# The first two images reordered, sums written into the low halves, and the middle products laid out row by row

## The chip, the cores and the metric

The kernel runs on one core of a Trainium2 chip. The metric is device time in microseconds for one call. Before the change three runs took 1633.83 to 1634.32 us, median 1634.29.

## The reference

The input x is (32, 256, 28, 28) in fp32. The reference convolves each channel with 12 fixed log-polar masks of 9x9, mixes the 12 results over the channels with a 4x3 convolution (`w_conv1`), adds a 1x1 convolution of x and a bias, normalizes over the batch, adds x and takes the ReLU:

```
xp  = log_pooling(x)                      # 12 mask averages per pixel, as (B, C, 4*H, 3*W)
out = conv(xp, w_conv1, stride (4, 3)) + conv1x1(x, w_center) + b_center
out = (out - mean(out, (0,2,3))) * rsqrt(var(out, (0,2,3)) + 1e-5) * gamma + beta
out = relu(out + x)
```

## The kernel before, in words

**Layout.** The 256 channels are two halves (c) of 128 partitions. A picture lies column by column: 28 columns of H = 28 values. An image is worked through in two halves, step s = 2 x image + c, and each output half o is accumulated in PSUM over both c. Odd and even columns of the output (q) have their own banks: banks 0 to 3 for y, banks 4 to 7 (MBANK on) for the middle products m = 0, 1 of each o. U = 14, HALF = U x H = 392.

**Sums.** VectorE builds for each half, in this order (`image_steps`, line 558): `d`, the differences of columns two apart (L567); D1 and D2, even plus odd and odd minus even columns (L570, L571); V, vertical sums of `d` (L573); then `row3` and `row3v` (L586, L590), `box4` and `box3` (L604, L606), and three pooled pairs: `pooled_sums` 0 and 1 (L610, L612) and the third in two pieces (`short_sum`, L617). row3 needs `row2`, the third pair needs `ends`: both are made by two transfers, a plain load issued by SP (`begin_sum`, L283) and an adding one issued by POOL (`add_from`, L246) that waits for it. The sums stand in buffers `inner` (D1, D2, V) and `pooled` (two slots).

**High and low parts.** Each fp32 operand is a rounded fp32r part plus a rest. ScalarE copies the sum into the first half of `inner_split` or `pooled_split`, which rounds it (`split_inner` L374, `split_pooled` L384); VectorE subtracts that from the sum and writes the rest into the second half (L582, L594 and `lo_of_pooled`, L553). Weights are split the same way (`split_weights`, `lo_of_weights`). A product is three matmuls: high x high, low weights x high, high x low (`products`, L669; L675 to L677).

**TensorE's order** per half (L686 to L731): the middle products of D1 and D2 (for each m, o: the tap in the middle on all 392 columns, and two shifted taps on 378), 36 matmuls; the inner products of V and `d`, 24 of 392 columns; three pooled pairs, 24 of 364 columns each. For c = 0 it waits for `middle_taken` ahead of the middle products and for `y_ready` ahead of the inner ones. It releases `m_done`, `inner_done` (once per half) and `pooled_done` (once per pair).

**The striped layout.** D1, D2 and the middle banks hold two columns interleaved, so that a shift by one row of the picture is a shift by 2 elements within a stripe of 56: 7 stripes of 54 elements are the shifted product. The column pairs are written by VectorE at a step of 2 elements:

```
striped = (STRIPE, STRIPES), (1, 2), (2, H)                 # 56 x 7, 1 x 2, 2 x 28
add(view(inner, D1, *striped), even, odd)
shorter = (STRIPE, STRIPES), (1, SHORTER)                   # 7 runs of 54
```

**Taking an image.** After the middle products of c = 1 ScalarE copies the banks of m = 0 to `m1_copy` (`copy_m1`, L391). In the next image VectorE's `take_middle` (L503) adds and subtracts them with the banks of m = 1, read from PSUM, into `y_stage`, right behind V of c = 0; `take_y` (L515) adds banks 0 to 3 after the first low pooled part. SP then saves y to DRAM (L312). ScalarE measures sum and sum of squares of each y half (`measure`, L398).

**The order on SP** per half (`image_steps`, L301): when row3 is ready, x of the next image; row2's load when the second pooled sum of this half is done; ends' load when the third is; for c = 0 the save of y. At the start: x, both blocks of the first half's weights, row2, ends, x of the second half, its weights, the parameters (L326 to L332). In images 0 and 1 the order is the loop's, with the weights' work put in; `transform_weights(0)` comes first of all. TensorE runs WARM_UP = 20 matmuls on zeros before (L682).

**The tail.** 32 images are finished in two rounds of 16 slots: y and x are loaded, VectorE scales and adds (L662), ScalarE adds the shift and takes the ReLU (L444), and stores. Slots 1 to 15 lie over the buffers of the conv stage, in places of 784 KB (`load_places`, L322), each loaded as soon as what stood there is done with: 4 in `w_stage` once the y save of image 30 has landed, 5 more in `w_first` after the last half but one, and so on (L338 to L350).

Of the kernel before, what the change touches and what calls it, by code (L numbers as in the profile page):

```python
# [7 lines left out]
def conv_bn_relu_program(nc, x, x_wide, w_raw, b_center, gamma, beta, out, y_dram):  # L8
# [22 lines left out]

    STRIPES, STRIPE = U // 2, 2 * H
    SHORTER = STRIPE - 2
# [34 lines left out]
    with ctx:  # L68
# [11 lines left out]
        with ExitStack() as phase1:  # L80
# [7 lines left out]
            w_stage = reused("w_stage", CH * RAW * CHANNELS)  # L88
            w_first = reused("w_first", 2 * TAPS * CHANNELS, F32R)
# [7 lines left out]
            inner = reused("inner", 4 * HALF)  # L97
            pooled = reused("pooled", 2 * PAIR)
# [8 lines left out]
        m1_copy = sb("m1_copy", CH * HALF)  # L107

        D1, D2, VD, SD = 0, HALF, 2 * HALF, 4 * HALF

# [19 lines left out]
        AFTER_STAGE = places_within("w_stage")  # L130
        AFTER_FIRST = places_within("w_first")
        AFTER_SUMS = places_within("pooled")
# [66 lines left out]
        m1_copied = sem("m1_copied")  # L199
# [15 lines left out]
        WARM_UP = 20  # L215
# [60 lines left out]
        def _(sp):  # L276
# [18 lines left out]
            def load_weights(c):  # L295
                for part, (first, end) in enumerate(((0, RAW_OUTER), (RAW_OUTER, RAW))):
                    sp.dma_start(view(w_stage, (c * RAW + first) * CHANNELS, (1, (end - first) * CHANNELS)),
                                 w_raw[:, c, first:end, :].rearrange("p k o -> p (k o)"))\
                        .then_inc(w_loaded[c][part], 16)
# [27 lines left out]
            load_weights(0)  # L327
            begin_sums(0, 0)
            load_x(0, 1)
            load_weights(1)  # L330
# [29 lines left out]
        def _(act):  # L360
# [13 lines left out]
            def split_inner(s):  # L374
                act.wait_ge(v_ready, s + 1)
                wait_from_one(act, inner_done, s)
                nc.scalar.activation(view(inner_split, 0, (1, SD)), view(inner, 0, (1, SD)), ACT.Copy)\  # L377
# [6 lines left out]
            def split_pooled(s, c, j):  # L384
                wait_from_one(act, pooled_done, PAIRS * s - PAIRS + j + 1)
# [22 lines left out]
            def image_steps(image, first=False):  # L408
                for c in range(CH):
                    s = CH * image + c  # L410
                    if c == 0 and not first:
                        copy_m1(image - 1)
# [7 lines left out]
                    for j in range(PAIRS):  # L420
                        split_pooled(s, c, j)
# [353 lines left out]
```

## Time and profile before

| | |
|---|---|
| three runs | 1633.83, 1634.29, 1634.32 us |
| the profiled execution | 1634.39 us, span of its instructions 1632.7 us |
| mean granted TensorE clock | 0.949 |
| TensorE busy | 1459.9 us, 89% |
| VectorE busy | 1421.4 us, 87% |
| ScalarE busy | 639.6 us, 39% |
| POOL busy | 121.3 us, 7% |
| moved by the transfer engines | 268.76 MB |

The profile is one execution recorded in the chip. Busy is the time in which an engine had an instruction running; matmuls overlap, so the distance from the start of one to the start of the next says more of their cost than the duration of one. Times within the trace are counted from the first instruction. The conv stage ends at 1480, the rest is the normalizing tail.

### The profile page before, as it was taken

To read this page: it belongs to the slowest core of one execution; us is meant where nothing else is said; L and a number is where in the kernel's file an instruction comes from. 1 tells how busy PE (TensorE), PEld (TensorE's weight loads), DVE (VectorE), ACT (ScalarE), POOL (GpSimd) and SP (SyncE) were. 2 spreads that over 40 slices of the span, in tenths; PEclk is the share of its full clock that TensorE was granted. 3 is DMA by queue.
4 is the path that set the end of the run, shared out by engine and by line. 5 is a ranking of instruction groups with operands and counts; after the bars stand their busy time and mean duration, and the time that the engine had idled before them with its cause. 6 is when DMAs were issued, how large, how long until landed. Compare 5 with 4: busy or idle time off the path is not lost.

```text
span 1632.7 us, 22865 instructions
## 1 busy us (share of the span) xinstructions
PE 1459.9 (89%) x8468; PEld 1458.6 (89%) x8468; DVE 1421.4 (87%) x1391; ACT 639.6 (39%) x689; POOL 121.3 (7%) x160
## 2 busy tenths in 40 slices
PE   6899999999999999999999999999999999992000
PEld 5899999999999999999999999999999999992000
DVE  7999999999999999999999999999999999986332
ACT  3334434334334343443433334343343333435332
POOL 1000000000000000000000000000000000000000
PEclk8999999999999999999999999999999999996555
DMA  6456554555555555455545555555555455579999
GB/s 200 108 132 146 136 134 126 125 145 127 119 124 133 145 136 137 128 122 143 135 115 120 136 139 136 141 127 128 135 136 122 116 140 133 136 253 420 425 425 400
DMA packets 65352, 268.76 MB, mean 165 GB/s; under 512 B 7616, under 2 KB 7616, under 8 KB 65344
## 3 DMA queue, kind: packets, MB, share of 16 engines
q1 hardware_dynamic: 39744, 160.53, 29.5%
q0 software_dynamic: 20736, 82.45, 26.5%
q10 hardware_dynamic: 4864, 25.69, 3.8%
q14 instruction: 6, 0.05, 0.0%
q8 instruction: 2, 0.03, 0.0%
HBM read 218.07 MB, written 50.58 MB: 165 GB/s over the span
## 4 chain that ended last, share of the span: by engine, by line
PE 86%; DMA 6%; DVE 3%; ACT 2%; another core or an unknown queue 1%; issue 1%; ACTq 0%; SPq 0%; DVEq 0%; POOLq 0%
PE acc L676 29%; PE acc L677 29%; PE acc L675 29%; DMA out<-phase 3%; DMA phase<-y_dram 2%; ACT phase L444 1%; DMA row<-x_wide 1%; DVE pooled L452 1%; DVE pooled_split L453 1%; DVE inner_split L453 0%; ACTq L447 0%; ACT m_copy L403 0%; DVE y_stage L452 0%; DVE row3v L452 0%
## 5 line engine op out<-in xcount | busy, mean ns | idle before, releaser
L387 ACT ACTIVATE pooled_split<-pooled 128x1456 fp32r<-128x1456 f32 x192 | 273.4, 1424 | 609.6 <-DVE pooled L452 609.6
L453 DVE TENSOR_TENSOR pooled_split<-pooled,pooled_split 128x1456 fp32r<-128x1456 f32 x192 | 315.1, 1668 | 0.3 <-ACT pooled_split L387 0.3
L675 PE MATMUL acc<-pooled_split,w_first 128*128 128x364 f32 x768 | 252.7, 329 | 5.1 <-DVE pooled_split L453 5.1
L676 PE MATMUL acc<-pooled_split,w_first 128*128 128x364 f32 x768 | 253.4, 330 | 0.0
L677 PE MATMUL acc<-pooled_split,w_first 128*128 128x364 f32 x768 | 253.4, 330 | 0.0
L677 PE MATMUL acc<-pooled_split,w_outer 128*128 128x364 f32 x768 | 252.8, 329 | 0.0
L676 PE MATMUL acc<-pooled_split,w_outer 128*128 128x364 f32 x768 | 252.5, 329 | 0.0
L675 PE MATMUL acc<-pooled_split,w_outer 128*128 128x364 f32 x768 | 252.0, 328 | 0.0
L675 PE MATMUL acc<-inner_split,w_first 128*128 128x392 f32 (+1 forms) x640 | 219.2, 342 | 13.6 <-DVE inner_split L453 9.3
L677 PE MATMUL acc<-inner_split,w_first 128*128 128x392 f32 (+1 forms) x640 | 218.3, 341 | 0.0
L676 PE MATMUL acc<-inner_split,w_inner 128*128 128x392 f32 (+1 forms) x640 | 218.0, 341 | 0.0
L676 PE MATMUL acc<-inner_split,w_first 128*128 128x392 f32 (+1 forms) x640 | 217.9, 340 | 0.0
L677 PE MATMUL acc<-inner_split,w_inner 128*128 128x392 f32 (+1 forms) x640 | 217.5, 340 | 0.0
L675 PE MATMUL acc<-inner_split,w_inner 128*128 128x392 f32 (+1 forms) x640 | 217.1, 339 | 0.0
L452 DVE TENSOR_TENSOR pooled<-box,row 128x1456 f32<-128x1456 f32 x128 | 208.2, 1667 | 0.0
L453 DVE TENSOR_TENSOR inner_split<-inner,inner_split 128x1568 fp32r<-128x1568 f32 x64 | 114.7, 1792 | 95.7 <-ACT inner_split L377 95.7
L377 ACT ACTIVATE inner_split<-inner 128x1568 fp32r<-128x1568 f32 x64 | 96.9, 1514 | 188.7 <-PE acc L677 167.8
L675 PEld LDWEIGHTS acc<-pooled_split,w_first 128*128 128x128 f32 x768 | 145.0, 189 | 5.4 <-DVE pooled_split L453 5.4
L676 PEld LDWEIGHTS acc<-pooled_split,w_first 128*128 128x128 f32 x768 | 144.7, 188 | 0.0
L677 PEld LDWEIGHTS acc<-pooled_split,w_first 128*128 128x128 f32 x768 | 144.7, 188 | 0.0
L676 PEld LDWEIGHTS acc<-pooled_split,w_outer 128*128 128x128 f32 x768 | 144.5, 188 | 0.0
L677 PEld LDWEIGHTS acc<-pooled_split,w_outer 128*128 128x128 f32 x768 | 144.4, 188 | 0.0
(82 smaller groups left out, 2154.9 us busy)
## 6 DMA issues: line engine op xcount, KB each, us to landing
row<-x_wide SPq DMA_DIRECT2D x64, 558.0 KB, 3.6
row<-x_wide POOLq DMA_DIRECT2D x64, 558.0 KB, 7.3
ends<-x_wide SPq DMA_DIRECT2D x64, 504.0 KB, 4.0
ends<-x_wide POOLq DMA_DIRECT2D x64, 504.0 KB, 5.8
x_pad<-x SPq DMA_DIRECT2D x64, 392.0 KB, 3.1
y_dram<-y_stage SPq DMA_DIRECT2D x31, 784.0 KB, 8.5
phase<-y_dram SPq DMA_DIRECT2D x30, 784.0 KB, 30.8
out<-phase ACTq DMA_DIRECT2D x30, 784.0 KB, 34.4
```

The source lines that it names most:

```text
L377: nc.scalar.activation(view(inner_split, 0, (1, SD)), view(inner, 0, (1, SD)), ACT.Copy)\
L387: nc.scalar.activation(view(pooled_split, 2 * j * PAIR, (1, PAIR)), view(pooled, (PAIRS * c + j) % 2 * PAIR, (1, PAIR)), ACT.Copy)\
L444: nc.scalar.activation(x_slot(d, o), x_slot(d, o), ACT.Relu, bias=bn_shift[:, o:o + 1]).then_inc(relu_done, 1)
L452: add = lambda out_, a, b: nc.vector.tensor_tensor(out_, a, b, ALU.add)
L453: sub = lambda out_, a, b: nc.vector.tensor_tensor(out_, a, b, ALU.subtract)
L675: nc.tensor.matmul(place, hi_w, hi_in, start=start, stop=False)
L676: nc.tensor.matmul(place, lo_w, hi_in, start=False, stop=False)
L677: return nc.tensor.matmul(place, hi_w, lo_in, start=False, stop=stop)
```

## The change

- **Layout.** D1, D2 and the middle banks are row by row: element (h, u) at 14 h + u. A shift by one row is a shift by 14, and a shifted product is one run of 378. VectorE writes D1 and D2 with a step of 14 elements.
- **Copies.** ScalarE copies all four middle banks (`copy_middle`, two instructions of 784 elements), reading PSUM with a step of 14 and writing columns to `m_copy`. `take_middle` is two instructions of 784 elements on SBUF. TensorE waits for `m_copied` in place of `middle_taken`.
- **Freed buffers.** `inner` and `pooled` are gone. Their sums are written into the low halves of `inner_split` and `pooled_split`, and the low part is formed in place. So VectorE waits for `inner_done` and for `pooled_done` of the half before ahead of writing. `spare`, of the same size, lies behind `w_stage`.
- **Order on VectorE.** Images 0 and 1 have orders of their own, with each low part right behind its sum. In the loop: (take_middle,) row3, row3v, boxes, differences, two pooled sums, the low parts of the inner sums, the first low pooled part, (take_y,) the third sum, two low parts.
- **SP.** The second weight block comes behind row2's load; x of the next image waits for V too; one place of the tail is loaded after image 29, two after image 30, and places 3 to 6 behind the last y save. WARM_UP is 70.

```
-    STRIPES, STRIPE = U // 2, 2 * H
-    SHORTER = STRIPE - 2
+    SHORTER = HALF - U
+            spare = reused("spare", 2 * PAIR + 4 * HALF)
-            inner = reused("inner", 4 * HALF)
-            pooled = reused("pooled", 2 * PAIR)
-        m1_copy = sb("m1_copy", CH * HALF)
+        m_copy = sb("m_copy", 2 * CH * HALF)
-        AFTER_STAGE = places_within("w_stage")
+        AFTER_STAGE = places_within("spare")
-        WARM_UP = 20
+        WARM_UP = 70
...
@@ SP
             load_x(0, 0)
-            load_weights(0)
-            begin_sums(0, 0)
+            load_weights(0, 0)
+            begin_sum(0, 0, row2, W + 3, row2_begun)
+            load_weights(0, 1)
+            begin_sum(0, 0, ends, W, ends_begun)
...
                         sp.wait_ge(row3_ready, CH * image + c + 1)
+                        sp.wait_ge(v_ready, CH * image + c + 1)
...
-            with sp.Fori(1, LAST) as image:
+            with sp.Fori(1, LAST - 2) as image:
                 image_steps(image)
+            image_steps(LAST - 2)
+            sp.wait_ge(w_lo_ready, CH * len(GROUPS))
+            sp.wait_ge(y_saved, 16 * (LAST - 3))
+            load_places(0, 1)
+            image_steps(LAST - 1)
+            load_places(1, 3)
             image_steps(LAST, last=True)
             sp.wait_ge(y_saved, 16 * LAST)
-            sp.wait_ge(w_lo_ready, CH * len(GROUPS))
-            load_places(0, AFTER_STAGE)
+            load_places(3, AFTER_STAGE)
@@ ScalarE
+            def copy_middle(image):
                 act.wait_ge(m_done, image + 1)
                 wait_from_one(act, y_measured, MOMENTS * image)
+                wait_from_one(act, middle_taken, image + FREE)
+                for m in range(2):
+                    nc.scalar.activation(view(m_copy, m * CH * HALF, (HALF, CH), (H, U), (1, H)),
+                                         view(acc, (MBANK + CH * m) * BANK, (BANK, CH), (1, U), (U, H)), ACT.Copy)\
+                        .then_inc(m_copied, 1)
@@ VectorE, the loop
+            def image_steps(image):
                 for c in range(CH):
                     s = CH * image + c
+                    if c == 0:
                         take_middle(image - 1)
+                    three_columns(image, c)
+                    boxes(s)
+                    differences(image, c)
+                    first_sum(s)
+                    second_sum(s)
+                    lo_of_sums(s)
+                    lo_of_shifted(s)
+                    lo_of_pooled(s, 0)
+                    if c == 0:
                         take_y(image - 1)
+                    third_sum(s)
+                    lo_of_pooled(s, 1)
+                    lo_of_pooled(s, 2)
@@ VectorE, the new functions
+            def pooled_place(s, j, first, *dims):
+                wait_from_one(dve, pooled_done, PAIRS * s - PAIRS + j + 1)
+                return view(phase2, POOLED_LOW + 2 * j * PAIR + first, *dims)
...
+            def differences(image, c):
...
+                sub(view(d03, 1, (U * TALL, 2), (TALL, U), (1, H)),
+                    columns(c, -1, 2, U, (H, 2)), columns(c, 1, 2, U, (H, 2))).then_inc(d_ready, 1)
...
+                wait_from_one(dve, inner_done, s)
+                add(view(phase2, INNER_LOW + D1, (1, U), (U, H)), even, odd)
+                sub(view(phase2, INNER_LOW + D2, (1, U), (U, H)), odd, even)
...
+            def first_image():
+                for c in range(CH):
+                    differences(0, c)
+                    transform_weights(c)
+                    lo_of_sums(c)
+                    lo_of_weights(c, range(INNER_GROUPS))
+                    lo_of_shifted(c)
+                    three_columns(0, c)
+                    boxes(c)
+                    first_sum(c)
+                    lo_of_weights(c, [FIRST_OUTER_GROUP - 1])
+                    lo_of_pooled(c, 0)
+                    second_sum(c)
+                    lo_of_weights(c, range(FIRST_OUTER_GROUP, len(GROUPS)))
+                    lo_of_pooled(c, 1)
+                    third_sum(c)
+                    lo_of_pooled(c, 2)
+            def second_image():
+                for c in range(CH):
+                    s = CH + c
+                    differences(1, c)
+                    if c == 0:
+                        take_middle(0)
+                    lo_of_sums(s)
+                    three_columns(1, c)
+                    if c == 0:
+                        take_y(0)
+                    lo_of_shifted(s)
+                    boxes(s)
+                    first_sum(s)
+                    lo_of_pooled(s, 0)
+                    second_sum(s)
+                    lo_of_pooled(s, 1)
+                    third_sum(s)
+                    lo_of_pooled(s, 2)
+                    if c == 0:
+                        make_pivot()
@@ TensorE
-                        pe.wait_ge(middle_taken, image + FREE)
+                        pe.wait_ge(m_copied, 2 * image + FREE)
...
-                            products(c, o, tap, view(acc, bank + 2, *shorter),
-                                     inner_split, data, INNER + data, *shorter)
+                            products(c, o, tap, view(acc, bank + U, (1, SHORTER)),
+                                     inner_split, data, INNER + data, (1, SHORTER))
```

## Rows read from the trace of the kernel before

**Rows 1.** The page's slices, 40 of 40.8 us: busy tenths of TensorE and the transfer engines.

```profile
PE   6899999999999999999999999999999999992000
...
DMA  6456554555555555455545555555555455579999
```

**Rows 2.** Timeline of TensorE: start us, duration us, line, instruction; half images and the ends.

```profile
121.87 0.34 PE L675 MATMUL acc<-inner_split,w_first 128*128 128x392 f32 x1
...
506.62 0.34 PE L675 MATMUL acc<-inner_split,w_inner 128*128 128x392 f32 x1
...
513.02 0.34 PE L675 MATMUL acc<-inner_split,w_inner 128*128 128x392 f32 x1
...
517.30 0.33 PE L675 MATMUL acc<-pooled_split,w_outer 128*128 128x364 f32 x1
...
529.27 0.34 PE L675 MATMUL acc<-inner_split,w_first 128*128 128x392 f32 x1
...
1479.70 0.32 PE L677 MATMUL acc<-pooled_split,w_outer 128*128 128x364 f32 x1
```

**Rows 3.** Timeline of SP: the last y save; and windows (columns: PE, PEld, DVE, ACT, POOL, PEclk, DMA, GB/s).

```profile
1439.78 0.43 SPq L312 DMA_DIRECT2D y_dram<-y_stage  x1
...
1500.00:1632.70 132.70, 0.00 (x0) 0.00 (x0) 50.70 (x52) 50.32 (x55) 8.75 (x16) 0.50 1.00 417
```

**Rows 4.** Timeline of VectorE in a half of image 14; then groups by line and form (busy us, mean ns).

```profile
677.52 1.79 DVE L453 TENSOR_TENSOR inner_split<-inner,inner_split 128x1568 fp32r<-128x1568 f32 x1 [1.78 <-ACT inner_split L377]
679.23 1.03 DVE L452 TENSOR_TENSOR row<-row,x_pad 128x840 f32<-128x840 f32 x1
...
681.27 0.97 DVE L453 TENSOR_TENSOR inner_split<-d,inner_split 128x784 fp32r<-128x784 f32 x1
...
684.20 3.25 DVE L452 TENSOR_TENSOR pooled<-box,row 128x1456 f32<-128x1456 f32 x2
...
L387 ACT ACTIVATE pooled_split<-pooled 128x1456 fp32r<-128x1456 f32 x192 | 273.4, 1424 | 609.6 <-DVE pooled L452 609.6
...
L452 DVE TENSOR_TENSOR inner<-x_pad 128x392 f32<-128x392 f32 x64 | 35.8, 559 | 0.0
L452 DVE TENSOR_TENSOR y_stage<-acc,m_copy 128x392 f32<-128x392 f32 x64 | 35.7, 558 | 1.1 <-ACT m_copy L394 1.1
...
L394 ACT ACTIVATE m_copy<-acc 128x784 f32<-128x784 f32 x32 | 26.5, 829 | 57.9 <-PE acc L677 57.9
```

**Rows 5.** Timeline of VectorE in the first three images; last, a transfer of the first 30 us.

```profile
6.28 0.42 DVE L471 SCALAR_TENSOR_TENSOR y_stage<-w_stage 128x256 f32<-128x256 f32 x1 [6.28 <-DMA w_stage<-w_raw]
...
19.21 1.03 DVE L452 TENSOR_TENSOR row<-row,x_pad 128x840 f32<-128x840 f32 x1 [2.41 <-DMA row<-x_wide]
...
109.81 0.97 DVE L453 TENSOR_TENSOR d<-x_pad 128x784 f32<-128x784 f32 x1
...
111.66 0.97 DVE L452 TENSOR_TENSOR inner<-d 128x784 f32<-128x784 f32 x1
...
row<-x_wide POOLq DMA_DIRECT2D x1, 558.0 KB, 9.0
```

**Rows 6.** Transfers: row2's load on SP, its add on POOL, and the add's median landing.

```profile
642.36 0.33 SPq L283 DMA_DIRECT2D row<-x_wide  x1
...
646.91 0.87 POOL L246 DMA_DIRECT2D row<-x_wide  x1 [13.74 <-DMA row<-x_wide]
...
row<-x_wide POOLq DMA_DIRECT2D x64, 558.0 KB, 7.3
```

**Rows 7.** Groups of POOL's memsets by form: busy us, mean ns.

```profile
L241 POOL MEMSET x_pad<- 128x56 f32 x2 | 0.3, 147 | 0.0
...
L241 POOL MEMSET row<- 128x30 f32 x1 | 0.2, 157 | 0.0
L241 POOL MEMSET std<- 128x2 f32 x1 | 0.1, 100 | 0.3 <-POOLq L766 0.3
```

**Rows 8.** Windows, the stretch behind TensorE's stop in image 1 (columns as in rows 3).

```profile
81.30:84.70 3.40, 3.40 (x11) 3.40 (x12) 3.40 (x4) 1.42 (x1) 0.86 (x1) 0.56 0.35 30
```

More of the change, by code:

```diff
@@ L293, in begin_sums, with load_weights @@
                 begin_sum(image, c, ends, W, ends_begun)
[L295 to L299, printed above, removed]
+            def load_weights(c, part):
+                first, end = ((0, RAW_OUTER), (RAW_OUTER, RAW))[part]
+                sp.dma_start(view(w_stage, (c * RAW + first) * CHANNELS, (1, (end - first) * CHANNELS)),
+                             w_raw[:, c, first:end, :].rearrange("p k o -> p (k o)"))\
+                    .then_inc(w_loaded[c][part], 16)
             def image_steps(image, first=False, last=False):
@@ L375, in split_inner @@
                 act.wait_ge(v_ready, s + 1)
[L376 to L377 removed]
+                nc.scalar.activation(view(inner_split, 0, (1, SD)), view(phase2, INNER_LOW, (1, SD)), ACT.Copy)\
                     .then_inc(inner_hi_ready, 1)
@@ L554, in lo_of_pooled @@
                 dve.wait_ge(pooled_hi_ready, PAIRS * s + j + 1)
-                sub(view(pooled_split, (2 * j + 1) * PAIR, (1, PAIR)), view(pooled, pooled_slot(c, j), (1, PAIR)),
-                    view(pooled_split, 2 * j * PAIR, (1, PAIR)).bitcast(F32)).then_inc(pooled_lo_ready, 1)
-            def image_steps(image, first=False, second=False):
+                sub(view(pooled_split, (2 * j + 1) * PAIR, (1, PAIR)),
+                    view(phase2, POOLED_LOW + 2 * j * PAIR, (1, PAIR)),
+                    view(pooled_split, 2 * j * PAIR, (1, PAIR)).bitcast(F32))\
+                    .then_inc(pooled_lo_ready, 1)
@@ new lines, in columns @@
+            def columns(c, first_column, step, n, *more):
+                return view(x_pad, c * X_PAD + (first_column + 2) * H, *more, (step * H, n), (1, H))
+            def differences(image, c):
+                s = CH * image + c
+                dve.wait_ge(x_loaded[c], 16 * (image + 1))
+                wait_from_one(dve, inner_lo_ready, 2 * s)
+                sub(view(d03, 1, (U * TALL, 2), (TALL, U), (1, H)),
+                    columns(c, -1, 2, U, (H, 2)), columns(c, 1, 2, U, (H, 2))).then_inc(d_ready, 1)
+                even, odd = (view(x_pad, c * X_PAD + (q + 2) * H, *every_other_column) for q in range(2))
+                wait_from_one(dve, inner_done, s)
+                add(view(phase2, INNER_LOW + D1, (1, U), (U, H)), even, odd)
+                sub(view(phase2, INNER_LOW + D2, (1, U), (U, H)), odd, even)
+                dve.wait_ge(d_ready, s + 1)
+                add(view(phase2, INNER_LOW + VD, (HALF, 2), (H, U), (1, H)),
+                    view(d03, 0, (U * TALL + 1, 2), (TALL, U), (1, H)),
+                    view(d03, 1, (U * TALL + 1, 2), (TALL, U), (1, H))).then_inc(v_ready, 1)
@@ new lines, in three_columns @@
+            def three_columns(image, c):
+                s = CH * image + c
+                dve.wait_ge(x_loaded[c], 16 * (image + 1))
+                dve.wait_ge(row2_ready, 16 * (s + 1))
+                add(view(row3, 1, (ROW3_H, W + 2), (1, H)), view(row2, 4, (ROW2_H, W + 2), (1, H)),
+                    columns(c, 0, 1, W + 2)).then_inc(row3_ready, 1)
+                dve.wait_ge(row3_ready, s + 1)
+                add(view(row3v, 2, (ROW3V_H, W + 2), (1, H + 1)), view(row3, 0, (ROW3_H, W + 2), (1, H + 1)),
+                    view(row3, 1, (ROW3_H, W + 2), (1, H + 1))).then_inc(row3v_ready, 1)
@@ L576, in image_steps @@
-                    if first:
-                        lo_of_weights(c, range(INNER_GROUPS))
-                    if c == 0 and not first:
-                        take_middle(image - 1)
-                    dve.wait_ge(inner_hi_ready, 2 * s + 1)
-                    sub(view(inner_split, INNER, (1, SD)), view(inner, 0, (1, SD)),
-                        view(inner_split, 0, (1, SD)).bitcast(F32)).then_inc(inner_lo_ready, 1)
-                    dve.wait_ge(row2_ready, 16 * (s + 1))
-                    add(view(row3, 1, (ROW3_H, W + 2), (1, H)), view(row2, 4, (ROW2_H, W + 2), (1, H)),
-                        columns(0, 1, W + 2)).then_inc(row3_ready, 1)
@@ L626, in _ @@
             dve.wait_ge(zeroed, ZEROED)
-            transform_weights(0)
-            image_steps(0, first=True)
-            image_steps(1, second=True)
+            first_image()
+            second_image()
             with dve.Fori(2, IMAGES) as image:
```

133 lines of the change are left out of this document (52 added, 81 removed).

## The prediction

> **What bounds the kernel now.** I read the page's slices first: TensorE is full from the second slice to the end of the conv stage [rows 1]. The timeline of TensorE says how full. Half an image lasts 22.65 us, 506.62 to 529.27: 36 middle products in 6.40, 24 inner in 4.28, 72 pooled in 11.97 [rows 2]. Image 2 starts at 121.87 and the last product at 1479.70, ending 0.33 later: 30 images at 45.27 us without a gap. So the conv stage ends at (start of image 2) + 30 x (one image), and after it the transfer engines are full to the last microsecond, 417 GB/s and a share of 1.00 [rows 3]. The end of the kernel is therefore the moment from which the tail loads may start, plus bytes over rate; TensorE matters because it sets that moment. VectorE is the second bound: in the halves shown it idles only 1.78 us, waiting for ScalarE's rounding [rows 4].
>
> The sum is made against the profiled execution: 1634.39 us, span 1632.7; the median of the runs is 1634.29, the same.
>
> **1. The middle products.** 48 per image stream 378 columns, as 7 runs of 54, and become one run. Now they cost (6.40 - 12 x 0.178)/24 = 177.5 ns apart, no less than the 178.3 of 392 columns, while 364 columns cost 166.3 [rows 2]. On the line between those two, 378 would be 172.3. Bounds: no gain (177.5), and the pitch of 364 (166.3). I take 172.3, since a plain run is what 392 is: 5.2 ns x 48 x 30 = **-7.5 us** after image 2; images 0 and 1 are set by VectorE.
>
> **2. When image 2 starts.** Both orders give VectorE the same list for images 0 and 1, so I move its clock. It starts image 2 at 109.81, having begun at 6.28 when the weights landed [rows 5].
> - Differences come before the weights' sums, so it starts when x has landed (between 3 and 6.28, ahead of the weights on the queue; I take 4.6): -1.7.
> - Waits removed: row2 2.41, one for rounding and one for image 2's sums, together 4.3: 109.81 - 1.7 - 4.3 = 103.8.
> - Each low part now stands right behind its own sum, so VectorE waits for ScalarE's copy of 1.42 plus two hand-overs of 0.04 and the lost overlap of 0.09: 1.6 [rows 4]. Image 1 has six, 9.6. In image 0 two of three have weights' low parts of 0.60 and 1.13 between: 2 x (1.0 + 0.5 + 1.6) = 6.1. In image 1, c = 1, the inner sums' low part waits likewise, 1.7.
> - row2 of image 0: its base load no longer queues behind the second block of weights (768 KB, about 1.9 us at the tail's rate), so the add goes out near 9.0, not 19.21 - 9.0 = 10.2, and lands 9.0 later [rows 5]. VectorE wants it after differences 2.7, the weights' sums 3.0, low part 1.7, five low parts of weights 3.0 and one more 0.9: 4.6 + 11.3 = 15.9: waits 2.0.
> Image 1 ends at 103.8 + 9.6 + 6.1 + 1.7 + 2.0 = 123.2. The loop's new order then puts three_columns, boxes, differences and two sums ahead of the low part that TensorE needs. row2 of image 2 is begun after the second sum of the half before, at about 115.3; the base load reaches POOL 4.55 later and the add takes 6.0 to 8.8, median 7.3 [rows 6]: 127. Then 4.1 (to the boxes), 2.7, 3.2 and 1.8 [rows 4, 5]: image 2's first product at 138.7.
>
> **3. The strided writes.** VectorE writes D1 and D2 with a hop of 56 bytes per element. At a hop of 8 bytes it pays nothing (392 elements in 559 ns [rows 4]). The far row is POOL's: a memset of 30 single elements at a hop of 124 bytes takes 157 ns, where a plain one, on the line through 2 elements in 100 and 56 in 147, would take 124: 1.1 ns more per element [rows 7]. Bounds 0 and about 0.4 us per write; the hop is nearer to the far row's kind (every element elsewhere), so I take 0.39: 8 writes ahead of image 2's products (those of the first half hide behind the row2 wait), +3.1, image 2 at 141.8. That is +19.9 against 121.87.
> The Trainium skill (Vector Engine (DVE) Microarchitecture Reference, "Measured stream behaviour on trn2") gives 2.50 ns for an output stepping 24 words every element against 1.05; by it a write costs 0.57 more, and the sum would be about 15 us higher, the third rival. Its demand for adjacent pairs of words does not hold in the row of the 8-byte hop.
>
> **4. The clock.** TensorE stands over 10 us before image 2. After its 4.6 us stop at 76.7 to 81.3 the granted clock was 0.56 for 3.4 us (the 1.2 GHz level) [rows 8]: +1.7, which later work no longer hides. WARM_UP 70 ends between 14 and 23 us; the first pooled products are VectorE's to release at 27, and the next half at 46, so it costs and brings nothing.
>
> **5. The loop afterwards.** The tight chain runs from the middle products of c = 1 to those of the next image: release 0.25, two copies of 0.83 overlapped to 1.6, take_middle 2 x 0.89, three_columns and boxes 4.1, differences 2.73, two sums 3.17, low part 1.79, hand-overs 0.1: 15.5 [rows 4, 5]. TensorE covers it with 4.28 + 11.97 = 16.25, less 0.18 for the early weight load: 0.58 to spare. Two hops of 0.39 overdraw it by 0.2; if the weight load needs no lead, by 0.02. I take 0.1 x 30 = **+3.0**. The other new wait, second_sum on P1 of the half before, leaves 11.97/3 = 3.99 against 0.25 + 1.58 + 1.79 + 0.05 = 3.67, just enough. row2 in the loop: begun at 2.0 before the half, landed 4.55 + 7 later, at +9.6, needed at +8.7 to +10: covered. ScalarE is 39% busy; its second copy of 0.83 costs only what the chain counts. The copy reads PSUM at a hop of 56 bytes; VectorE reads PSUM at 8 bytes at full rate (558 ns for 392 [rows 4]), and I take 0.
>
> **6. The tail.** The loads wait for the last y save. It was issued at 1439.78, 5.2 after image 31 began (121.87 + 29 x 45.27) [rows 2, 3]; now it stands behind the third sum, 5.9 after the image's start: **+0.7**. Three places of 784 KB load beside images 30 and 31, where the transfer share is about half [rows 1], instead of in the full stretch: 3 x 784 KB at 420 GB/s = **-5.7**. The bytes that are left stay enough to keep the engines full until the scaling begins.
>
> **Sum**: 1634.4 + 19.9 + 1.7 - 7.5 + 3.0 + 0.7 - 5.7 = 1646.5, say **1646** (own range 1640 to 1653).
>
> **Rivals.**
> - *Free hops* (0.15). No 3.1 in the head, no 3.0 in the loop: 1640. For: the 8-byte row. Against: POOL's.
> - *Faster* (0.10). Hops are free, the 378-column products fall to 166.3 (another 6.0 ns x 1440 = -8.6), and the clock is not lowered (-1.7): 1630. It decides from a pitch under about 167. Against: more columns than 364.
> - *Dear hops* (0.15). At 1.5 ns per element a write costs 0.59: head +1.6, loop (1.18 - 0.58) x 30 = 18 instead of 3: 1663.
> - *ScalarE pays too* (0.12). At 1.0 ns per element its two copies cost 1.6 us per image in the same chain, 47 in all: 1693. Advanced Engine Details and Errata of the Trainium skill ("Memory Cachelines") has PSUM lines of 8 bytes; it speaks of matmuls, and VectorE's read of one word per 8 bytes shows no cost.
> - *The change does not do what it says* (0.11). The products in one run stay at 177.5, as their cost may not lie in the runs: +7.5, 1654. If instead the early places only displace other loads, +5.7.
> The forecast has 0.37.
>
> **The numbers.** The range 1632 to 1673 leaves out the faster end and ScalarE's, about 0.2. A measurement tells 0.2% (3.3 us) from nothing: faster is below 1631, same reaches to 1637.6. Faster 0.11; same 0.14, from the low ends of the forecast and of free hops; slower 0.75.
>
> **What would show it.** Right: 128x392 writes near 0.95 us; 36 middle products in about 6.27; image 2's first product near 142 after a stop of over 10 us and a lowered clock; waits of 1.6 us of VectorE on ScalarE all through image 1; 3 loads of phase2 before the last image; a full transfer share from the last y save. Wrong: the writes still at 0.56; ScalarE's copies from PSUM well over 0.83; TensorE standing in each image for more than 0.2 us; image 2 starting before 130, which would turn the sign.

## The result, and the profile after

| | before | after |
|---|---|---|
| median of the runs | 1634.10 us (4 runs) | 1649.01 us (4 runs, 1648.69 to 1649.38) |
| profiled execution, its span | 1634.39, 1632.7 us | 1649.38, 1647.7 us |
| mean granted TensorE clock | 0.949 | 0.947 |

The ratio is 1.0091, 95% interval 1.0074 to 1.0109: slower by 14.9 us. The forecast was 1646 us, within 1632 to 1673, with 0.75 on slower.

The page's slices of the changed kernel, 40 of 41.2 us (before: [rows 1]):

```profile
PE   9887999999999999999999999999999999994000
...
DMA  6335555555555555554555555555545555579999
```

TensorE is fed less densely in the second to fourth slice and is full for the rest. The shape behind the head (all up to image 2's start) is that of before, shifted. So the timeline of TensorE says what the conv stage lost. It answers to [rows 2]: image 2's start, the seam ahead of image 14 in the loop (where TensorE goes over from one image to the next), the last product.

```profile
128.98 0.32 PE L739 MATMUL acc<-pooled_split,w_outer 128*128 128x364 f32 x1
140.28 0.69 PE L737 MATMUL acc<-inner_split,w_first 128*128 128x392 f32 x1 [10.97 <-DVE inner_split L464]
...
670.10 0.34 PE L737 MATMUL acc<-inner_split,w_inner 128*128 128x392 f32 x1
...
686.19 0.32 PE L739 MATMUL acc<-pooled_split,w_outer 128*128 128x364 f32 x1
686.46 0.45 PE L737 MATMUL acc<-inner_split,w_first 128*128 128x392 f32 x1
686.75 0.34 PE L738 MATMUL acc<-inner_split,w_first 128*128 128x392 f32 x1
...
1501.76 0.32 PE L739 MATMUL acc<-pooled_split,w_outer 128*128 128x364 f32 x1
```

Image 2 starts at 140.28 instead of 121.87, after a stop of 10.97 us that the trace lays on VectorE's low part. The last product ends at 1502.08 instead of 1480.02. Of these 22.06 us 18.41 are there before image 2, and the rest is in 30 images. TensorE doesn't run through the seam at 686: from the last pooled product to the first of the middle it is 0.27, from there to the second 0.29, where an unbroken stream (the lines of e2 below) has 0.17 and 0.18. That is 0.21 us at each of the 29 seams behind image 2; ahead of image 15 it is once 0.22 more. The line at 670.10 is the first inner product of the half before, from which step 5 below counts.

The windows behind the stop (columns: PE, PEld, DVE, ACT, POOL, PEclk, DMA share, GB/s), answering to [rows 8]:

```profile
140.20:143.60 3.40, 3.32 (x10) 3.33 (x11) 3.40 (x4) 0.00 (x0) 0.67 (x1) 0.50 0.35 141
143.60:147.00 3.40, 3.40 (x14) 3.40 (x14) 3.40 (x4) 0.93 (x1) 0.19 (x1) 0.63 0.76 110
```

The clock is at its 1.2 GHz level for the first 3.4 us and comes back in the next. The first 60 products of image 2 (the middle and inner ones of c = 0) take 13.30 us, those of an image in the loop 10.7: 2.6 us for the clock.

VectorE in image 14's first half, the timeline (answering to [rows 4]):

```profile
672.20 0.98 DVE L463 TENSOR_TENSOR y_stage<-m_copy 128x784 f32<-128x784 f32 x1 [1.50 <-ACT m_copy L406]
673.09 0.97 DVE L464 TENSOR_TENSOR y_stage<-m_copy 128x784 f32<-128x784 f32 x1
...
679.07 0.87 DVE L463 TENSOR_TENSOR phase<-x_pad 128x392 f32<-128x392 f32 x1
679.77 0.89 DVE L464 TENSOR_TENSOR phase<-x_pad 128x392 f32<-128x392 f32 x1
680.48 0.99 DVE L463 TENSOR_TENSOR phase<-d 128x784 f32<-128x784 f32 x1
681.36 3.26 DVE L463 TENSOR_TENSOR phase<-box,row 128x1456 f32<-128x1456 f32 x2
684.53 1.80 DVE L464 TENSOR_TENSOR inner_split<-phase,inner_split 128x1568 fp32r<-128x1568 f32 x1
```

This is the chain of the prediction's step 5, and nothing in it is idle between 672.20 and TensorE's restart at 686.46. A strided write takes 0.70 from its start to the next start (679.07, 679.77, 680.48), a plain one 0.48 (675.03 to 675.51 in the trace of e2). The groups by line and form have the duration of such a write, and of ScalarE's copies:

```profile
L463 DVE TENSOR_TENSOR phase<-x_pad 128x392 f32<-128x392 f32 x64 | 55.3, 864 | 0.0
...
L406 ACT ACTIVATE m_copy<-acc 128x784 f32<-128x784 f32 x64 | 49.2, 822 | 43.5 <-PE acc L739 43.5
```

and the list of waits (total, times, longest):

```profile
DVE y_stage L463 <- ACT m_copy L406: 44.6, 30, 1.5
DVE phase L463 <- PE acc L739: 31.6, 31, 2.3
```

ScalarE reads PSUM at a hop of 56 bytes in 822 ns, against 829 contiguous. In each of the 30 images VectorE stands 1.5 us for it: it reaches `take_middle` before the middle products of c = 1 are done and copied, so it can't work ahead, and the chain from there on is all that TensorE waits for. The second line is the wait that the freed buffers brought: in image 13, c = 1, VectorE stands 0.97 us for TensorE ahead of its second pooled sum (at 660.03). The 1.50 ahead of 672.20 comes behind it, so VectorE has more slack in that half than this wait takes, and it costs TensorE nothing.

The tail, from SP's timeline (answering to [rows 3]): three places before the last image, then the save and what follows it.

```profile
1392.96 0.45 SPq L319 DMA_DIRECT2D phase<-y_dram  x1
...
1438.21 0.68 SPq L322 DMA_DIRECT2D phase<-x  x1
1438.94 0.57 SPq L319 DMA_DIRECT2D phase<-y_dram  x1
...
1462.89 0.50 SPq L315 DMA_DIRECT2D y_dram<-y_stage  x1
1468.79 0.33 SPq L322 DMA_DIRECT2D phase<-x  x1
```

Before, the save went out at 1439.78 [rows 3], and the loads began here:

```profile
1448.19 0.33 SPq L316 DMA_DIRECT2D phase<-y_dram  x1
```

The save is 23.1 later, the loads only 20.6, since it lands in 5.9 instead of 8.4. The total grew by 15.0. So 5.6 of the 20.6 come back in the tail, which is near what e1 measures for the early places.

### The profile page after: what moved, and what is told of

Its sections match the earlier page's. It is cut to its first block, busy times and chain, and to the rows that moved or that the text cites. A ratio compares the mean times of both kernels' runs of the same rounds, so it can differ in the third digit from the quotient of the medians.

```text
span 1647.7 us, 22775 instructions
## 1 busy us (share of the span) xinstructions
PE 1473.7 (89%) x8518; PEld 1463.6 (89%) x8518; DVE 1449.7 (88%) x1327; ACT 648.3 (39%) x721; POOL 121.2 (7%) x160
## 4 chain that ended last, share of the span: by engine, by line
PE 81%; DVE 5%; ACT 5%; ACTq 4%; DMA 2%; issue 2%; SPq 0%; DVEq 0%; POOLq 0%
PE acc L737 27%; PE acc L738 27%; PE acc L739 27%; ACTq L458 4%; ACT phase L455 3%; DMA row<-x_wide 2%; DVE phase L463 2%; ACT pooled_split L397 1%; DVE box L463 1%; DVE inner_split L464 0%; DVE row L463 0%; DVE row3v L463 0%; DVE pooled_split L464 0%; DVE d L464 0%; ACT m_copy L415 0%
## 5 line engine op out<-in xcount | busy, mean ns | idle before, releaser
L397 ACT ACTIVATE pooled_split<-phase 128x1456 fp32r<-128x1456 f32 x192 | 266.1, 1415 | 329.3 <-DVE phase L463 329.3
L464 DVE TENSOR_TENSOR pooled_split<-phase,pooled_split 128x1456 fp32r<-128x1456 f32 x192 | 315.8, 1671 | 14.5 <-ACT pooled_split L397 14.5
L388 ACT ACTIVATE inner_split<-phase 128x1568 fp32r<-128x1568 f32 x64 | 97.1, 1517 | 512.9 <-DVE phase L463 512.9
L463 DVE TENSOR_TENSOR phase<-box,row 128x1456 f32<-128x1456 f32 x128 | 211.3, 1673 | 31.6 <-PE acc L739 31.6
L737 PEld LDWEIGHTS acc<-pooled_split,w_outer 128*128 128x128 f32 x768 | 144.2, 188 | 0.6 <-DVE pooled_split L464 0.6
L738 PEld LDWEIGHTS acc<-pooled_split,w_outer 128*128 128x128 f32 x768 | 144.5, 188 | 0.0
L739 PEld LDWEIGHTS acc<-pooled_split,w_outer 128*128 128x128 f32 x768 | 144.4, 188 | 0.0
```

Source lines behind the costliest of these rows:

```text
L388: nc.scalar.activation(view(inner_split, 0, (1, SD)), view(phase2, INNER_LOW, (1, SD)), ACT.Copy)\
L397: nc.scalar.activation(view(pooled_split, 2 * j * PAIR, (1, PAIR)), view(phase2, POOLED_LOW + 2 * j * PAIR, (1, PAIR)), ACT.Copy)\
L463: add = lambda out_, a, b: nc.vector.tensor_tensor(out_, a, b, ALU.add)
L464: sub = lambda out_, a, b: nc.vector.tensor_tensor(out_, a, b, ALU.subtract)
L737: nc.tensor.matmul(place, hi_w, hi_in, start=start, stop=False)
L738: nc.tensor.matmul(place, lo_w, hi_in, start=False, stop=False)
```

## The experiments

Each was timed beside the kernel before on the same chip. The times of before in these four groups of runs have medians of 1634.1 to 1634.7 us, so a difference between times of two groups is good to some 0.6 us. The diffs of e1, e2, e3, f1, f2, g2 and h1 are against the changed kernel, unless another is named.

**e1: without the early places.**

```
-            image_steps(LAST - 2)
...
-            load_places(0, 1)
-            image_steps(LAST - 1)
-            load_places(1, 3)
...
-            load_places(3, AFTER_STAGE)
+            load_places(0, AFTER_STAGE)
```

> The changed kernel with its tail loads as before: no place before the last y save, all seven behind it. If the three early places are worth their bytes (3 x 784 KB at 420 GB/s), 5.7 us more than the changed kernel's 1649.0: 1654.7. If they only displaced other loads: 1649.

1654.24 us (1653.13 to 1654.54), ratio 1.012 [1.0103, 1.0137]. As expected (1654.7): the early places are worth 5.2 by the two times, 4.6 by what each is above its own times of before.

**e2: contiguous writes of D1 and D2.** The values then stand elsewhere than the products expect them; the amount of work is the same.

```
-                add(view(phase2, INNER_LOW + D1, (1, U), (U, H)), even, odd)
+                add(view(phase2, INNER_LOW + D1, (H, U), (1, H)), even, odd)
```

(and D2 likewise)

> The changed kernel, with D1 and D2 written column by column at a step of one element (the values stand elsewhere, so the middle products are of other elements; every count and size is kept). Theory: each write falls from 0.86 to 0.56 us (0.22 between starts), the head gains 8 x 0.22 = 1.8, and TensorE's two delays of 0.11 ahead of each image's first middle products vanish, 30 x 0.22 = 6.7: 1640.5. Rival, the delay is that of the wait of the second sum on the half before: only the head's 1.8, 1647.

1640.63 us (1640.32 to 1640.97), ratio 1.0038 [1.0024, 1.0053]: 8.4 less. The group of the writes:

```profile
L463 DVE TENSOR_TENSOR phase<-x_pad 128x392 f32<-128x392 f32 x64 | 35.8, 560 | 0.0
```

and TensorE's timeline at image 2's start and at the seam of a later image:

```profile
138.82 0.69 PE L737 MATMUL acc<-inner_split,w_first 128*128 128x392 f32 x1 [9.94 <-DVE inner_split L464]
...
681.67 0.33 PE L739 MATMUL acc<-pooled_split,w_outer 128*128 128x364 f32 x1
681.84 0.34 PE L737 MATMUL acc<-inner_split,w_first 128*128 128x392 f32 x1
682.02 0.34 PE L738 MATMUL acc<-inner_split,w_first 128*128 128x392 f32 x1
```

and VectorE's low part ahead of that seam:

```profile
679.65 1.78 DVE L464 TENSOR_TENSOR inner_split<-phase,inner_split 128x1568 fp32r<-128x1568 f32 x1
```

Two writes, each 0.22 shorter, leave the chain with 0.44 less, and the seam closes: an image takes 45.08 instead of 45.30 from start to start, 6.4 over 29 seams, and 1.5 are gained in the head (138.82 against 140.28; 1.8 forecast). So the loop's stall comes from the hops, and without them the chain fits. By how much the low part shows: it ends at 681.43, 0.41 ahead of the product at 681.84, where in the changed kernel it ends at 686.33 and TensorE restarts 0.13 later.

**e3: image 1's low pooled parts one step later**, so that VectorE has a sum to make while ScalarE rounds.

```
                     first_sum(s)
+                    second_sum(s)
                     lo_of_pooled(s, 0)
-                    second_sum(s)
+                    third_sum(s)
                     lo_of_pooled(s, 1)
-                    third_sum(s)
                     lo_of_pooled(s, 2)
```

> The changed kernel, in image 1 alone the second pooled sum ahead of the first low part, and the third ahead of the second. Theory: VectorE's waits of 1.49 for ScalarE go (6 of them, 9 us), and the second sum of the last half, from which row2 of image 2 is begun, comes 7.6 earlier; image 2's first product near 132.7, not 140.3: 1641.4. Rival, the loop's order sets the time and the head is hidden: 1649.

1640.52 us (1639.73 to 1641.14), ratio 1.0038 [1.0023, 1.0052]: 8.5 less. VectorE's timeline in image 1, c = 0, first of the changed kernel:

```profile
80.85 1.67 DVE L463 TENSOR_TENSOR phase<-box,row 128x1456 f32<-128x1456 f32 x1
84.01 1.68 DVE L464 TENSOR_TENSOR pooled_split<-phase,pooled_split 128x1456 fp32r<-128x1456 f32 x1 [1.49 <-ACT pooled_split L397]
85.60 1.67 DVE L463 TENSOR_TENSOR phase<-box,row 128x1456 f32<-128x1456 f32 x1
```

then of e3:

```profile
81.20 3.25 DVE L463 TENSOR_TENSOR phase<-box,row 128x1456 f32<-128x1456 f32 x2
84.37 1.67 DVE L464 TENSOR_TENSOR pooled_split<-phase,pooled_split 128x1456 fp32r<-128x1456 f32 x1
85.95 1.74 DVE L463 TENSOR_TENSOR phase<-box,ends 128x728 f32<-128x728 f32 x2
87.61 3.25 DVE L464 TENSOR_TENSOR pooled_split<-phase,pooled_split 128x1456 fp32r<-128x1456 f32 x2
```

The same instructions, with the six waits of 1.49 gone. Image 2 starts at 131.76: 8.5 of its 18.4 came from having each low part right behind its own sum.

**e4: the kernel before, with the layout and the two copies alone** (diff against the kernel before).

```
-                    add(view(inner, D1, *striped), even, odd)
+                    add(view(inner, D1, (1, U), (U, H)), even, odd)
...
-                            products(c, o, tap, view(acc, bank + 2, *shorter),
-                                     inner_split, data, INNER + data, *shorter)
+                            products(c, o, tap, view(acc, bank + U, (1, SHORTER)),
+                                     inner_split, data, INNER + data, (1, SHORTER))
```

(with `copy_middle`, the two-instruction `take_middle` and the wait for `m_copied` of the change)

> The kernel before with the row-by-row layout and the two copies alone: its order, its buffers, 20 warm-up matmuls, no early places. Theory: 48 products of 172.5 instead of 177.3 ns, 32 images: -7 us; the strided writes cost VectorE 0.45 per half, which its waits of 1.5 to 1.8 per half for ScalarE absorb, save 1 us in the first images: 1634.1 - 7 + 1 = 1628. Rival, the layout itself costs in the loop (writes, copies): 1634 or more.

1630.13 us (1629.75 to 1630.6, 9 runs), ratio 0.9973 [0.9963, 0.9983]: by itself this part is a gain, of 4.6 where about 6 were expected. TensorE's timeline, image 2's start and the last product:

```profile
123.80 0.34 PE L673 MATMUL acc<-inner_split,w_first 128*128 128x392 f32 x1
...
1476.03 0.32 PE L675 MATMUL acc<-pooled_split,w_outer 128*128 128x364 f32 x1
```

An image takes (1476.35 - 123.80)/30 = 45.09 instead of 45.27, with no stop: 5.5 less in 30 images, where 7 were expected in 32. Image 2 starts 1.9 later than in the kernel before (1 was expected). The writes have the hop here too (863 ns in the group), but in this order TensorE never waits for VectorE from image 2 on.

**f1: the layout taken out of the changed kernel.**

```
-                add(view(phase2, INNER_LOW + D1, (1, U), (U, H)), even, odd)
+                add(view(phase2, INNER_LOW + D1, *striped), even, odd)
```

(and the products, the one copy by ScalarE, and four instructions in `take_middle`, as in the kernel before)

> The changed kernel with the striped layout, one copy of the middle banks by ScalarE and four instructions in take_middle again; the new order of the first images, the freed buffers, the strided-free copies' absence and the early places of the tail stay. Theory (the head costs about 20, the row-by-row layout is worth about nothing net: the products give about 6, the writes at a hop of 56 bytes and the stalls ahead of the middle products take about 8): the middle products cost 6.37 to 6.40 us per half again without stalls, image 2 starts near 139, time 1646 to 1648, a little faster than the changed kernel or the same. Rival (the layout is where the loss is): 1640 or less.

1646.36 us (1645.63 to 1646.37), ratio 1.0074 [1.0057, 1.0091]: 2.7 less than the changed kernel. The same edit that gains 4 to 5 us in the kernel before (e4) costs 2.7 in the changed one: without it image 2 starts at 138.92 and an image takes 45.27 with no stall, so the cheaper products (5.5 in 30 images) are less than what the hops cost at the seams and in the head. All else in the change together, the new orders and freed buffers less what the earlier start and the early places give, costs 12.2.

**f2: e3, and image 2 in image 1's order too**, so that the loop's order begins at image 3.

```
-            second_image()
-            with dve.Fori(2, IMAGES) as image:
+            early_image(1)
+            early_image(2)
+            with dve.Fori(3, IMAGES) as image:
                 image_steps(image)
```

> As e3 (image 1's low pooled parts one step later), and image 2 in image 1's order too, so that the loop's order, which puts three sums ahead of TensorE's first low part, begins with image 3. Theory (the stop ahead of image 2 is the price of entering the loop's order, and VectorE gains on TensorE with each image): the stop moves to image 3 and shrinks to about 3 us, with little or no lowered clock behind it, so about 4 less than e3: 1636.5. Rival (VectorE is as fast as TensorE in these images, so the stop only moves): 1640.5, as e3.

1639.84 us (1637.97 to 1640.42), ratio 1.0035 [1.0023, 1.0048]. TensorE's timeline:

```profile
122.88 0.34 PE L738 MATMUL acc<-inner_split,w_first 128*128 128x392 f32 x1
...
175.59 0.69 PE L738 MATMUL acc<-inner_split,w_first 128*128 128x392 f32 x1 [7.46 <-DVE inner_split L464]
```

The rival was right in the time (the execution in the profile, 1637.97, is the fastest of six). Image 2 starts at 122.88 without a stop, and the stop stands ahead of image 3: 7.8 us from the product before it to the first one behind it, 7.2 ahead of image 2 in e3. It is the entry into the loop's order that costs, wherever it comes, and VectorE had gained nothing in the image between.

**g2: e3, and in the loop the inner low parts ahead of the two pooled sums.**

```
+                    lo_of_sums(s)
+                    lo_of_shifted(s)
                     first_sum(s)
                     second_sum(s)
-                    lo_of_sums(s)
-                    lo_of_shifted(s)
```

> As e3 (image 1's low pooled parts one step later), and in the loop the low parts of the inner sums ahead of the first and second pooled sums, in place of behind them. Theory (what stands ahead of the first low part, 3.2 us of pooled sums, makes the stop ahead of image 2 and the stalls of 0.22 in each image): the stop of 7.2 falls by 3.2 less a new wait of about 1.5 for ScalarE's rounding, the stalls go (6.5 in all), about 1632. Rival (VectorE has no room for one more wait of 1.5 in each half, so TensorE stands elsewhere in each image): 1640 or more.

1886.27 us (1882.09 to 1889.22), ratio 1.1543 [1.1525, 1.1562]. The rival's "1640 or more" covers the number, but neither theory had the reason. From the list of VectorE's waits:

```profile
DVE row L463 <- DMA row<-x_wide: 220.5, 61, 5.9
```

and the timelines of VectorE, SP and POOL, put in one order, for one turn of a circle:

```profile
656.61 1.03 DVE L463 TENSOR_TENSOR row<-row,x_pad 128x840 f32<-128x840 f32 x1 [2.74 <-DMA row<-x_wide]
...
668.27 3.25 DVE L463 TENSOR_TENSOR phase<-box,row 128x1456 f32<-128x1456 f32 x2
...
671.70 0.33 SPq L285 DMA_DIRECT2D row<-x_wide  x1
...
676.06 0.87 POOL L248 DMA_DIRECT2D row<-x_wide  x1 [22.43 <-DMA row<-x_wide]
...
684.96 1.03 DVE L463 TENSOR_TENSOR row<-row,x_pad 128x840 f32<-128x840 f32 x1 [5.26 <-DMA row<-x_wide]
```

The circle: row2 of the next half is loaded when the second pooled sum of this one is done (671.5), arrives 13.5 us later (684.96), and only then can VectorE begin the row whose pooled sums release the next load. It goes from transfer to transfer: 28.35 us from row add to row add here, and by the y saves of SP's timeline (1426.03, 1479.95) 53.9 per image, where TensorE needs 45.1. So the pooled sums can't simply be put off in this order: row3 stands first in it and waits for the transfer that they release.

**h1: the changed kernel, with image 1's order (as in e3) for every image.**

```
+            early_image(1, pivot=True)
+            with dve.Fori(2, IMAGES) as image:
+                early_image(image)
```

> The changed kernel with its layout, copies, freed buffers and early places, and with image 1's order (its low pooled parts one step later, as in e3) for every image: the differences and the low part of the inner sums first, the row sums and the pooled sums behind them, which is nearly the order of the kernel before. Theory (it is the loop's new order that costs: 7.2 to 7.8 where it is entered, a lowered clock behind it, and 0.22 in each image): image 2 starts near 123 as in f2, nothing stops later, and 1640.5 - 8.8 - 6.6 = 1625; perhaps 1.5 less, since the y save comes sooner in the image. Rival (without the second buffers of its own, VectorE waits for TensorE or ScalarE in this order, and each image stretches): 1635 or more.

1629.28 us (1628.62 to 1630.35, 8 runs), ratio 0.9969 [0.9959, 0.998]: 19.7 less than the changed kernel, with all of it but the order of images 1 to 31. 1625 was expected. The inner low parts stand ahead of the pooled sums here as in g2, but so do the differences ahead of row3: between the end of the sums (672.10) and the next row add (685.06, no wait) VectorE has 13 us of other work, which is what the transfer of row2 takes. No gap over 0.5 us is left from image 2 on, which starts at 123.07; the last product ends at 1475.62. TensorE did 1.7 better than expected (its last product ends 17.1 before that of e3, where 8.8 + 6.6 were expected), the tail did not. SP's timeline:

```profile
1442.52 0.44 SPq L315 DMA_DIRECT2D y_dram<-y_stage  x1
1448.24 0.33 SPq L322 DMA_DIRECT2D phase<-x  x1
```

Image 31 starts at 1430.39, and the save goes out 12.1 later, since on SP it queues behind `ends`, and so behind the third sum, which comes late. In the changed kernel it is 6.2 (1456.74 to 1462.89). These 6 us, less the 1.7, are the missing 4: before the save the transfer engines have little to do (a share of 0.25 from 1435.0 to 1442.5), and from 1448.2 on they are full.

**f3: e4, and the part of the new head that starts VectorE early** (diff against e4).

```
-            load_weights(0)
-            begin_sums(0, 0)
+            load_weights(0, 0)
+            begin_sum(0, 0, row2, W + 3, row2_begun)
+            load_weights(0, 1)
+            begin_sum(0, 0, ends, W, ends_begun)
...
+                        if c == 0:
+                            transform_weights(0)
...
+                    if first and c == 0:
+                        dve.wait_ge(inner_hi_ready, 2 * s + 2)
+                        low_of_shifted()
+                        lo_of_weights(c, range(FIRST_OUTER_GROUP - 1, len(GROUPS)))
                     dve.wait_ge(row2_ready, 16 * (s + 1))
```

(and ScalarE splits the first half's weights behind its inner sums)

> The kernel e4 (the kernel before with the row-by-row layout and the two copies alone) with the part of the new head that starts VectorE early: the second block of weights loaded behind row2, the differences ahead of the weights' sums, the weights' low parts ahead of row3 in the first half. Orders of image 1 and the loop stay those of before. Theory (the head of the kernel before loses 1.7 at the start, 2.4 waiting for row2): VectorE is about 4 us earlier in images 1 and 2, TensorE stops less, 1625 to 1626. Rival (the adding load of row2 lands no sooner, VectorE waits for it all the same): 1630, as e4.

1626.94 us (1626.67 to 1627.39), ratio 0.9957 [0.9941, 0.9974]: 3.2 less than e4, 22.1 less than the changed kernel. VectorE's timeline, answering to [rows 5]:

```profile
4.24 0.98 DVE L457 TENSOR_TENSOR d<-x_pad 128x784 f32<-128x784 f32 x1 [4.24 <-DMA x_pad<-x]
...
19.36 1.03 DVE L456 TENSOR_TENSOR row<-row,x_pad 128x840 f32<-128x840 f32 x1
```

The row add starts where it did (19.36 against 19.21), but it has no wait ahead, and the work that used to follow it is done. Image 2 starts at 119.93, 3.9 before that of e4, and image 2 itself takes 0.6 longer than the 45.08 of those behind it.

**f4: f3 with a longer warm-up.**

```
-        WARM_UP = 20
+        WARM_UP = 60
```

> As f3 with WARM_UP 60 instead of 20. Theory (VectorE sets when the later products of the first half may run, so a faster first 36 products only stop longer): as f3, within 0.5 us. Rival (the clock of the first products counts): 1 to 1.5 us less than f3.

1626.87 us (1626.32 to 1627.05), ratio 0.9955 [0.9939, 0.9972]: as f3. The first 36 products take 7.8 us instead of 8.6, TensorE stops 2.95 instead of 2.08 before the pooled ones, and the longer warm-up brings nothing.

**g1: f3 with the early places** of the tail (the edit of e1, the other way).

> The kernel f3 (before, with the row-by-row layout, the two copies and the part of the new head that starts VectorE early) plus the early places of the tail: one after image 29, two after image 30. Theory (in the changed kernel the early places were worth 5.2 with nothing else tied to them): 1626.9 - 5.2 = 1621.7. Rival (in the changed kernel they fell on stretches with fewer demands on the transfer engines; here they delay row2 or only displace other loads): 1625 or more.

1626.48 us (1626.38 to 1626.7), ratio 0.9954 [0.994, 0.9967]: half a microsecond, which is no more than the groups differ by, where 5.2 were expected. The rival had the time, but not the reason. A window of g1 from the save's landing on, columns as above:

```profile
1442.60:1450.60 8.00, 8.00 (x50) 8.00 (x49) 7.97 (x8) 2.31 (x4) 0.00 (x0) 1.00 0.46 136
```

and of f3, from its save's landing to the same moment:

```profile
1441.20:1450.60 9.40, 9.40 (x58) 9.40 (x57) 9.37 (x9) 3.54 (x7) 0.00 (x0) 1.00 0.98 326
```

Without the freed buffers only four places are free when the save lands. With three of them loaded before, one is left: the transfer engines fall to a share of 0.46 and 136 GB/s until the next buffers come free at 1450.6. What was saved behind the last image was lost in front of it. In the changed kernel `spare` makes room for three more: seven places are free then, four of them are left to load, and the 5.2 of e1 are real. There too a dip is left, 0.88 and 327 GB/s from 1479.5 to 1486.0, where e1 has 1.02 and 425.

## Why the prediction was right

**What bounds the kernel.** Right: time = image 2's start + 30 images + the full tail. TensorE's end moved by 22.06 = 18.41 (start) + 2.6 (clock) - 5.5 (products) + 6.6 (stalls: 29 x 0.22, and 0.22 once), and the tail gave 7.1 back.

**Step 1, the products: right in kind, 2.0 too high.** -7.5 was forecast from 5.2 ns each. The image without stalls is 45.09 instead of 45.27 (e4), so 0.185 x 30 = -5.5, 3.9 ns each. My 177.5 was read in a half of c = 1; in those of c = 0 the 36 took 6.37 in the kernel before, 176.4 each. The 172.3 for one run was right (6.28 for the 36, so (6.28 - 12 x 0.178)/24 = 172.7).

**Step 2, the head: right.** 138.7 without the hops, 138.82 in e2. Its terms stood each by itself: six waits of 1.49 in image 1 (1.6 forecast), 1.58 for the inner sums (1.7), waits of 2.51 and 2.06 for row2 in images 0 and 2 (2.0 for both), VectorE at image 2's list at 123.96 (123.2). e3 took the six waits away and got 8.5 back (9.6 forecast for them). What I had not said, and f2 shows, is that the longer list ahead of the first low part is a price of the loop's order itself: 7.2 to 7.8 us of stop wherever it is entered. h1, which never enters it, has no stop from image 2 on.

**Step 3, the hop: in the middle of my bounds.** 0.22 per write (0.70 against 0.48 from start to start), where I took 0.39 from POOL's memset, near the upper one. So the price was mis-sized by 0.17. In the head 1.5 us (138.82 to 140.28) where I had 3.1. The Trainium skill's 2.50 ns per element (Vector Engine (DVE) Microarchitecture Reference, "Measured stream behaviour on trn2") is for a step of 24 words; here, at 14 words, 0.70 us for 392 elements is 1.79 ns. Its 1.45 over a plain stream is 0.56 here.

**Step 4, the clock.** +1.7 forecast, +2.6 measured: I priced the longer stop like the one of 4.6 us, but behind it the granted clock was 0.50 for 3.4 us and still 0.63 for the next. The first 36 products lost 1.7 behind the stop of e3 (7.2 us from product to product), 2.1 behind that of e2 (10.3), and 2.6 here (11.3).

**Step 5, the loop: the right chain, its slack mis-sized.** With hops of 0.39 I had it overdrawn by 0.02 to 0.2 and took 0.1. Measured, with hops of only 0.22, it takes 16.36 from the first inner product (670.10) to the restart (686.46), where TensorE's work lasts 16.25, and the product behind the restart is late by as much again: 0.21 in all. Without the two hops the chain is 15.92, not my 15.5. The 0.4 lie in small pieces: 0.1 more to the release and 0.15 more from the copies to `take_middle`, 0.1 in the rows and boxes, the rest in the hand-over to TensorE. So its slack without hops is about 0.3 (16.25 - 15.92; 0.41 - 0.13 in e2), not 0.58. Two errors of opposite sign left stalls of 6.6 instead of 3.0, and e2, where they are gone, ties them to the chain. The wait of the second sum that I had as just enough falls in c = 1, is 0.97 and costs nothing.

**Step 6, the tail.** The save lands in 5.9 instead of 8.4. So its loads moved by 20.6, 1.5 less than TensorE's end, where I had 0.7 more. The places: 5.2 by e1, 5.7 forecast.

**The sum.** Forecast 1646.5, measured 1649.0 to 1649.4. The errors of products (+2.0), stalls (+3.6) and clock (+0.9) are partly paid by image 2 starting 1.5 sooner and by the save (-2.2). The direction and most of the size rest on step 2, and step 2 was right. That the sum is within 3 us is in part luck: errors of 6.5 one way met 3.7 the other, and I had not foreseen the save's quicker landing.

**The rivals.** *Free hops* and *dear hops* are both out (e2). *ScalarE pays too* is out: 822 ns. *Faster* failed at the clock and at the pitch, 172.7. *The change does not do what it says* is out: the products got cheaper (e4), and the early places don't only displace other loads (e1); g1 shows when they do. e4 and h1 show besides that the change's parts can be had as a gain, without its order.

## What to carry to other kernels

- Price an edit in the place where it stands. The same layout gains 4 to 5 us where TensorE never waits for VectorE in the loop (e4), and costs 2.7 where the writes lie on the chain between them (the changed kernel against f1).
- Before an operation is put later in a loop, look at which transfer waits for it, and follow that transfer around to the operation itself. Circles do not show in a list of busy times. In g2 two low parts put ahead of two sums cost 246 us (against e3).
- An early transfer helps only if there is enough left to transfer when it would have been: count the bytes that may go in each stretch (g1 against e1).

## What was not expected of the hardware

- ScalarE reads PSUM at a hop of 56 bytes per element as fast as contiguously: 822 and 829 ns for 784 elements, and writes it contiguously. VectorE's write at the same hop costs 0.56 ns more per element.
- A matmul in 7 runs of 54 columns is not free. The 36 middle products take 6.37 to 6.40 us in stripes and 6.28 with runs of 378. The moving operand and the output in PSUM have the runs both, and no run here separates them.
- The same save of 784 KB landed in 8.4 us in the kernel before and in 5.7 to 5.9 us in the changed one and in h1. It holds for all 31 saves: the median landing is 8.5 us before, 5.7 in the changed kernel, 5.5 in h1. The transfer engines were as busy in both stretches (0.86 and 0.87), but moved 1.9 MB in the 8.4 us (225 GB/s) and 1.6 MB in the 5.9 (271 GB/s). So what else runs beside the save differs; which of it holds the save up stays open.

The fastest kernels measured are g1, f4 and f3, 1626.5 to 1626.9 us: 7 to 8 less than before, 22 less than the changed kernel. Not tried: h1 with the save ahead of `ends` on SP, and h1 with f3's head.
